# A gated cross-attention and expert layer on one core: from the fourth quad on the third product goes ahead of the fourth, and VectorE's last sums and ScalarE's second Silu take the same order

## The chip, the core and the metric

The kernel runs on one core of one Trainium2 chip. The metric is the device time of one execution in microseconds (us). Engines are named as the profile names them: PE is TensorE's matmul (PEld its weight load), DVE is VectorE, ACT is ScalarE, POOL is GpSimd, SP is SyncE, which issues the transfers.

## The reference

```python
x = x + tanh(g_xattn) * xattn(layernorm(x), ctx, wq, wk, wv, wo)   # x: 8 x 256 x 512
x = x + tanh(g_ffn) * ffn(layernorm(x), ...)
# ffn, N = 2048 tokens, G = 8 groups, inner width 352, hidden width 512:
xg = x[:, None, :] + einsum('ngi,ghi->ngh', soft, mask_up_w)
g = einsum('ngh,gih->ngi', xg, gate_proj_w)
u = einsum('ngh,gih->ngi', xg, up_proj_w)
a = silu(g) * u
d = einsum('ngi,ghi->ngh', a, down_proj_w)
y = einsum('ng,ngh->nh', scalar, d)
```

The attention part and the routing (softmax over 64 experts, the best 8, shares within each group) come first and are not touched. The change lies in the feed-forward part, in the two projections `g` and `u`, in `silu(g) * u`, and around the projection back (`down`).

## The kernel before

**Tiling.** Every fp32 product is made of three matmuls on a high and a low part of each operand (hi by lo, lo by hi, hi by hi). The feed-forward part goes over the 2048 tokens in two passes of 1024. In each pass it goes through 11 units of inner rows, and each unit is two quads (`j` = 0 and 1), so there are 44 quads, q = 0 to 43: the first pass has q 0 to 21, the second q 22 to 43. Even quads have `j` = 0, odd ones `j` = 1. The first and last two quads are also special in places.

**One quad.** Gate and up projections of 128 inner rows and two 512-token halves are computed with seven block products (a Strassen-like scheme) in place of eight. Each product is six matmuls of 128x512; four times a quad, one more matmul (`soft_product`) adds the group's mask part. The products collect in three PSUM banks A, B, C (banks 2, 3, 0 for even q, and 1, 4, 5 for odd q). PE's order in a quad is: product 1 (A), product 6 (B), the mask products (C, first pass only), product 2 (A), product 5 (C), product 7 (B), two soft matmuls (C, A), two `down` groups of six matmuls each ("early" ones, for all quads but q 0 to 2 and q 43), product 4 and its soft matmul (B), product 3 and its soft matmul (C), and the rest of the quad's four `down` groups. Product 4 waits for DVE's third sum (`s_s3`, "sum3"), product 3 for the sum after it (`s_c22`).

**DVE in a quad** (`for quad in quads` of the vector block), with the lines of the profile: `second_sum` (L1393, needed by product 7), in the first pass the mask tile `a_tile` (L1354, L1357, L1363, L1365, needed by product 5 and by the soft matmuls), the third sum (L1432), `c22` (L1439), the early residual additions `add_down` (L1381, one per `down` group; it frees bank 6 or 7), in the first pass pieces of the routing and of the second pass's token sums (L1385), then `c21` (L1486, needs product 4), `prod` (L1491), the first `scaled` (L1374), `c12` (L1498, needs product 3), `add_down`, `second_activations` (L1400 and the second L1374, which need the second Silu), and the fourth `add_down`, here or after the next quad's `second_sum`.

**ACT in a quad**: `first_sum` (L959), the high part of the previous quad's second activation block (`act_high`, L928), in even quads the high part of the previous unit's down weights (`down_weights`, L942), the next quad's weights in three groups (`weight_high`, L823: after product 2, after product 7, and group C after product 3), the first Silu (L1020), the second Silu (L1042, after `c12`) and `act_high` of the first block (L928).

**POOL in a quad**: in even quads the low parts of the previous unit's down weights (L716), then the low parts of the previous quad's two activation blocks (`act_low`, L721), the low parts of the next quad's weights (L670) in the three groups, and four sums of the weights of the quad after (L659 to L664). In a `down` group PE reads both parts of both quads' activation blocks of a unit: in an even quad the first early `down` is the first to read the unit that has just ended, and waits for POOL's down weights and for `act_low` of the odd quad's first block:

```python
                if t == 0:
                    pe.wait_ge(s_wd_lo, 2 * u + 2)
                if t % 4 == 0:
                    pe.wait_ge(s_at_lo, 4 * u + 2 + c + 1)
                if n >= 2:
                    pe.wait_ge(s_res, n - 1)
```

All order is written out by hand, engine by engine, with semaphores between engines. No scheduler moves anything.

## Time and profile before

| | before |
|---|---|
| median of 3 runs (lowest, highest) | 1060.4 us (1060.38, 1063.29) |
| the profiled execution: its own time, its span | 1062.4 us, 1060.6 us |
| granted TensorE clock | 0.998 |
| busy: PE, DVE, POOL, ACT | 99%, 70%, 58%, 37% of the span |
| chain that ended last, by engine | PE 86%, DVE 10% |

The profiled execution is one run, 2.0 us above the median of the others; its span is the time from its first to its last instruction. A row of the timeline gives start and duration in us, the engine, the line, the operation, and in brackets how long the engine was idle before it and for whom it waited. Matmuls of 128x512 follow each other every 0.23 us although each is shown with 0.39 us, since they are pipelined.

### The profile page before, as it was taken

What the parts mean: (1) busy time and instruction counts of PE and PEld (TensorE: products, weight loads), DVE (VectorE), ACT (ScalarE), POOL (GpSimd) and SP (SyncE); (2) the same over time, 40 slices, a digit from 0 to 9 for tenths busy, and PEclk for the clock granted to TensorE, in tenths of its full rate; (3) what the DMA queues carried; (4) which work ended last, traced back from release to release, by engine and by line L of the source; (5) the groups of instructions that cost most, each with busy time, mean ns of one, the idle gap of its engine ahead of it and who ended that gap; (6) DMA issues with size and microseconds to landing.
All of it is one profiled execution on the core that took longest, in us unless ns stands there. A gap on an engine that the chain in (4) does not pass through costs nothing.

```text
span 1060.6 us, 14525 instructions
## 1 busy us (share of the span) xinstructions
PE 1048.0 (99%) x5394; PEld 890.6 (84%) x5394; DVE 746.3 (70%) x1315; ACT 389.5 (37%) x651; POOL 616.2 (58%) x545
## 2 busy tenths in 40 slices
PE   8999999999999999999999999999999999999998
PEld 8989988988988888888877888888888888888887
DVE  7874655676677887788798888765566565666655
ACT  5334324334434435343334342333332333332331
POOL 2112102122435986778877987777668677668661
PEclk9999999999999999999999999999999999999999
DMA  9212226255796305124236323593321211221202
GB/s 331 77 40 99 61 50 150 61 135 144 239 245 201 129 28 73 53 76 38 92 117 77 123 97 99 179 290 110 115 75 48 75 62 41 75 75 47 75 28 80
DMA packets 114277, 111.64 MB, mean 105 GB/s; under 512 B 20896, under 2 KB 96672, under 8 KB 114208
## 3 DMA queue, kind: packets, MB, share of 16 engines
q1 hardware_dynamic: 113840, 110.58, 36.3%
q8 instruction: 43, 0.70, 0.3%
q14 instruction: 26, 0.21, 0.1%
q10 hardware_dynamic: 368, 0.15, 0.1%
HBM read 79.05 MB, written 31.65 MB: 104 GB/s over the span
## 4 chain that ended last, share of the span: by engine, by line
PE 86%; DVE 10%; issue 2%; ACT 1%; DMA 1%; SPq 0%; DVEq 0%
PE bank L89 37%; PE bank L1728 32%; PE bank L1541 9%; PE bank L1734 4%; PE bank L1560 2%; DVE tmp L1374 1%; DVE a_stack L1365 1%; PE bank L1742 1%; DVE a_stack L1363 1%; DVE xres L1381 1%; DVE a_tmp L1357 1%; DVE tmp L1491 1%; PE bank L1612 1%; DVE tmp L1400 1%; DMA w_raw<-in_w_qkvo 1%
## 5 line engine op out<-in xcount | busy, mean ns | idle before, releaser
L1728 PE MATMUL bank<-x2t,wgu_hi 128*128 128x512 f32 x1144 | 353.0, 390 | 0.0
L670 POOL TENSOR_TENSOR wgu_lo<-wgu_raw,wgu_hi 128x768 fp32r<-128x768 f32 (+2 forms) x143 | 216.7, 1527 | 79.3 <-ACT wgu_hi L823 77.9
L1728 PEld LDWEIGHTS bank<-x2t,wgu_hi 128*128 128x128 f32 x1144 | 214.9, 188 | 44.3
L1728 PE MATMUL bank<-x2t,wgu_lo 128*128 128x512 f32 x572 | 224.4, 392 | 1.1 <-DVE tmp L1432 0.8
L823 ACT CAST wgu_hi<-wgu_raw 128x512 fp32r<-128x512 f32 (+1 forms) x129 | 93.6, 726 | 223.1 <-PE bank L1734 185.3
L1381 DVE TENSOR_TENSOR xres<-xres,bank 128x512 f32<-128x512 f32 x175 | 119.4, 683 | 49.8 <-PE bank L89 49.3
L89 PE MATMUL bank<-wd_hi,at_second 128*128 128x512 f32 x336 | 130.8, 389 | 0.0
L1728 PEld LDWEIGHTS bank<-x2t,wgu_lo 128*128 128x128 f32 x572 | 107.4, 188 | 24.7 <-issue 1.6
L1374 DVE TENSOR_TENSOR tmp<-tmp,scalars 128x512 f32<-128x512 f32 x88 | 101.9, 1158 | 3.0
L642 POOL TENSOR_TENSOR kt_lo<-ctxt_raw,kt_hi 128x256 fp32r<-128x256 f32 x32 | 23.4, 764 | 137.6 <-ACT kt_hi L831 137.6
L89 PE MATMUL bank<-wd_hi,at_first 128*128 128x512 f32 x256 | 100.0, 390 | 0.7 <-issue 0.5
L716 POOL TENSOR_TENSOR wd_lo<-wd_raw,wd_hi 128x512 fp32r<-128x512 f32 x42 | 54.5, 1317 | 59.5 <-ACT wd_hi L942 59.5
L1432 DVE TENSOR_TENSOR tmp<-tmp,bank 128x512 f32<-128x512 f32 x44 | 30.2, 686 | 71.6 <-PE bank L1728 71.2
L89 PEld LDWEIGHTS bank<-wd_hi,at_second 128*128 128x128 f32 x336 | 63.1, 188 | 13.3
L1541 PE MATMUL bank<-xnt_hi,w_hi_qkv 128*128 128x256 f32 x256 | 72.5, 287 | 1.5 <-ACT xnt_hi L773 1.5
L1541 PE MATMUL bank<-xnt_hi,w_lo_qkv 128*128 128x256 f32 x256 | 72.5, 288 | 0.0
L1541 PE MATMUL bank<-xnt_lo,w_hi_qkv 128*128 128x256 f32 x256 | 68.4, 286 | 0.0
L1734 PE MATMUL bank<-soft_t,a_stack 128*128 128x512 f32 x176 | 62.6, 396 | 3.8 <-DVE a_stack L1365 3.7
L1020 ACT ACTIVATE tmp<-bank 128x512 f32<-128x512 f32 x44 | 26.4, 599 | 108.0 <-PE bank L1734 108.0
L89 PE MATMUL bank<-wd_lo,at_second 128*128 128x512 f32 x168 | 65.4, 389 | 0.0
L721 POOL TENSOR_TENSOR at_second<-tmp,at_second 128x512 fp32r<-128x512 f32 x44 | 60.1, 1386 | 5.7 <-ACT at_second L928 5.7
L721 POOL TENSOR_TENSOR at_first<-tmp,at_first 128x512 fp32r<-128x512 f32 x33 | 45.1, 1367 | 24.6 <-ACT at_first L928 24.6
(219 smaller groups left out, 2252.3 us busy)
## 6 DMA issues: line engine op xcount, KB each, us to landing
wgu_raw<-in_w_gate_up SPq DMA_DIRECT2D x43, 512.0 KB, 4.1
wd_raw<-in_w_down SPq DMA_DIRECT2D x22, 512.0 KB, 5.0
a_stacks<-a_stack SPq DMA_DIRECT2D x22, 192.0 KB, 1.9
a_stack<-a_stacks SPq DMA_DIRECT2D x22, 192.0 KB, 4.0
ctxt_raw<-in_ctx_t SPq DMA_DIRECT2D x8, 512.0 KB, 11.7
ctx_raw<-in_ctx SPq DMA_DIRECT2D x8, 512.0 KB, 8.5
x<-x_raw SPq DMA_DIRECT2D x8, 512.0 KB, 8.2
sums_raw<-x SPq DMA_DIRECT2D x16, 256.0 KB, 3.5
```

The source lines that it names most:

```text
L89: last = nc.tensor.matmul(out, stationary, moving, start=n == 0, stop=n == len(pairs) - 1)
L670: last = nc.gpsimd.tensor_tensor(wgu_lo[:, part], raw_of(quad)[:, part], f32(wgu_hi[:, part]), ALU.subtract)
L716: nc.gpsimd.tensor_tensor(lo[:, j], wd_raw[:, j], f32(hi[:, j]), ALU.subtract).then_inc(s_wd_lo, 1)
L721: nc.gpsimd.tensor_tensor(lo, tmp[quad.set][:, SUM_3 if c else ACTED], f32(hi), ALU.subtract).then_inc(s_at_lo, 1)
L823: nc.scalar.copy(wgu_hi[:, group], raw_of(quad)[:, group]).then_inc(s_fw_hi, 1)
L1020: nc.scalar.activation(sums[:, ACTED], psum_a[:], ACT.Silu).then_inc(s_silu_0, 1)
L1374: nc.vector.tensor_tensor(part, part, scalars[:, quad.j, c], ALU.mult).then_inc(s_act, 1)
L1381: nc.vector.tensor_tensor(row, row, bank[6 + t % 2][:], ALU.add).then_inc(s_res, 1)
L1432: nc.vector.tensor_tensor(sums[:, SUM_3], sums[:, SUM_1], psum_b[:], ALU.add).then_inc(s_s3, 1)
L1541: last = nc.tensor.matmul(bank[b0 + e // 2][:, (e % 2) * S:(e % 2 + 1) * S], stationary, moving, start=n == 0, stop=n == len(pairs) - 1)
L1728: last = nc.tensor.matmul(out_bank[:], stationary, moving, start=begins and n == 0, stop=n == len(pairs) - 1, skip_group_check=True)
L1734: return nc.tensor.matmul(out_bank[:], a_stack[:, quad.j, m, :], soft_t[:, quad.j, c, :], start=False, stop=True, skip_group_check=True)
```

## The change

From q = 3 on, PE does product 3 ahead of product 4. DVE's `c12` goes ahead of its `c21`, and ACT's second Silu ahead of the cast of weight group C. What waited for the end of product 3 as the quad's last product now waits for both. `act_high` of the first block comes last in all these quads.

```diff
+def third_first(q):
+
+    return q >= 3
...
                     sp.wait_ge(s_m3, q)
+                    sp.wait_ge(s_m4, q)
...
                 if q == QUADS - 1:
                     down_weights(UNITS - 1)
+                if third_first(q):
+                    second_silu()
                 if after:
                     eng.wait_ge(s_m3, q + 1)
+                    eng.wait_ge(s_m4, q + 1)
                     weight_high(after, 2, GROUP_C)
-                if quad.j == 1:
+                if third_first(q):
                     act_high(quad, 0)
-                eng.wait_ge(s_c12, q + 1)
-                nc.scalar.activation(sums[:, SUM_2], sums[:, SUM_2], ACT.Silu).then_inc(s_silu_1, 1)
-                if quad.j == 0:
-                    act_high(quad, 0)
+                else:
+                    if quad.j == 1:
+                        act_high(quad, 0)
+                    second_silu()
+                    if quad.j == 0:
+                        act_high(quad, 0)
...
                 if q >= 2:
                     dve.wait_ge(s_m3, q - 1)
+                    dve.wait_ge(s_m4, q - 1)
...
+                def last_sum():
+                    dve.wait_ge(s_m3, q + 1)
+                    nc.vector.tensor_tensor(sums[:, SUM_2], sums[:, SUM_2], psum_c[:], ALU.add).then_inc(s_c12, 1)
+
+                if third_first(q):
+                    last_sum()
                 dve.wait_ge(s_m4, q + 1)
                 nc.vector.tensor_tensor(sums[:, SUM_1], sums[:, SUM_1], psum_b[:], ALU.add).then_inc(s_c21, 1)
...
-                dve.wait_ge(s_m3, q + 1)
-                nc.vector.tensor_tensor(sums[:, SUM_2], sums[:, SUM_2], psum_c[:], ALU.add).then_inc(s_c12, 1)
+                if not third_first(q):
+                    last_sum()
...
             def product_3(quad):
                 q, psum_c = quad.q, banks_of(quad)[2]
+                pe.wait_ge(s_fw_lo, 3 * q + 3)
                 pe.wait_ge(s_c22, q + 1)
...
+                if third_first(q):
+                    product_3(quad)
                 product_4(quad)
-                product_3(quad)
+                if not third_first(q):
+                    product_3(quad)
```

On DVE this stood between the end of quad 41's early additions and quad 42's `second_sum` (tmp_1 holds the sums of odd quads, xres the output rows, bank4 is B and bank5 is C):

```order
L1486 TENSOR_TENSOR tmp_1_141<-tmp_1_141,bank4 128x512 [waits m4_ready]
L1491 TENSOR_TENSOR tmp_1_141<-tmp_1_141 128x512 [waits silu0_done,c21_done]
L1374 TENSOR_TENSOR tmp_1_141<-tmp_1_141,scalars_149 128x512 [waits prod_done]
L1498 TENSOR_TENSOR tmp_1_141<-tmp_1_141,bank5 128x512 [waits m3_ready]
L1381 TENSOR_TENSOR xres_49<-xres_49,bank6 128x512 [waits down_ready]
L1400 TENSOR_TENSOR tmp_1_141<-tmp_1_141 128x512 [waits c22_done,silu1_done]
L1374 TENSOR_TENSOR tmp_1_141<-tmp_1_141,scalars_149 128x512 [waits prod_done]
L1393 TENSOR_TENSOR tmp_0_140<-tmp_0_140,bank3 128x512 [waits m6_ready,sum1_done]
```

and this stands there now:

```order
L1503 TENSOR_TENSOR tmp_1_141<-tmp_1_141,bank5 128x512 [waits m3_ready]
L1508 TENSOR_TENSOR tmp_1_141<-tmp_1_141,bank4 128x512 [waits m4_ready]
L1513 TENSOR_TENSOR tmp_1_141<-tmp_1_141 128x512 [waits silu0_done,c21_done]
L1390 TENSOR_TENSOR tmp_1_141<-tmp_1_141,scalars_149 128x512 [waits prod_done]
L1397 TENSOR_TENSOR xres_49<-xres_49,bank6 128x512 [waits down_ready]
L1416 TENSOR_TENSOR tmp_1_141<-tmp_1_141 128x512 [waits c22_done,silu1_done]
L1390 TENSOR_TENSOR tmp_1_141<-tmp_1_141,scalars_149 128x512 [waits prod_done]
L1409 TENSOR_TENSOR tmp_0_140<-tmp_0_140,bank3 128x512 [waits m6_ready,sum1_done]
```

The sum that reads bank5 (`c12`) has moved from the fourth place to the first, and the two scaled products (`prod`, `scaled`) begin one place later, behind the end of product 4, which is now the quad's last.

On ACT, from quad 41's group C weights on to the down weights of quad 42 (at_second0 and at_second1 are the two activation blocks of an odd quad), before:

```order
L823 CAST wgu_hi_118<-wgu_raw1_145 128x768 [waits wgu_sums,m7_ready]
L823 CAST wgu_hi_118<-wgu_raw1_145 128x512 [waits wgu_sums,m3_ready]
L928 CAST at_second0_155<-tmp_1_141 128x512 [waits down_ready,act_ready]
L1042 ACTIVATE tmp_1_141<-tmp_1_141 128x512 [waits c12_done]
L959 COPY tmp_0_140<-bank2 128x512 [waits prod_done,m1_ready]
L928 CAST at_second1_156<-tmp_1_141 128x512 [waits down_ready,act_ready]
L942 CAST wd_hi_150<-wd_raw_147 128x512 [waits down_ready,wd_in]
L942 CAST wd_hi_150<-wd_raw_147 128x512
```

and now:

```order
L829 CAST wgu_hi_118<-wgu_raw1_145 128x768 [waits wgu_sums,m7_ready]
L1042 ACTIVATE tmp_1_141<-tmp_1_141 128x512 [waits c12_done]
L829 CAST wgu_hi_118<-wgu_raw1_145 128x512 [waits wgu_sums,m4_ready,m3_ready]
L934 CAST at_second0_155<-tmp_1_141 128x512 [waits down_ready,act_ready]
L965 COPY tmp_0_140<-bank2 128x512 [waits prod_done,m1_ready]
L934 CAST at_second1_156<-tmp_1_141 128x512 [waits down_ready,act_ready]
L948 CAST wd_hi_150<-wd_raw_147 128x512 [waits down_ready,wd_in]
L948 CAST wd_hi_150<-wd_raw_147 128x512
```

The Silu moved from behind the first block's cast to ahead of group C. The order of the four rows from L959 (L965 now) on is the same.

On PE, in quad 43, the last one, which has no early `down` groups, before (bank4 is B, bank5 is C):

```order
L1734 MATMUL bank5<-soft_t_146,a_stack_148 128x512 [waits a_loaded1]
L1734 MATMUL bank1<-soft_t_146,a_stack_148 128x512
L1728 MATMUL bank4<-x2t_139,wgu_lo_119 128x512 [waits sum3_done,wgu_lo_done]
L1728 MATMUL bank4<-x2t_139,wgu_hi_118 128x512 x2
L1728 MATMUL bank4<-x2t_139,wgu_lo_119 128x512
L1728 MATMUL bank4<-x2t_139,wgu_hi_118 128x512 x2
L1734 MATMUL bank4<-soft_t_146,a_stack_148 128x512
L1728 MATMUL bank5<-x2t_139,wgu_lo_119 128x512 [waits c22_done]
L1728 MATMUL bank5<-x2t_139,wgu_hi_118 128x512 x2
```

and now:

```order
L1756 MATMUL bank5<-soft_t_146,a_stack_148 128x512 [waits a_loaded1]
L1756 MATMUL bank1<-soft_t_146,a_stack_148 128x512
L1750 MATMUL bank5<-x2t_139,wgu_lo_119 128x512 [waits c22_done,wgu_lo_done]
L1750 MATMUL bank5<-x2t_139,wgu_hi_118 128x512 x2
L1750 MATMUL bank5<-x2t_139,wgu_lo_119 128x512
L1750 MATMUL bank5<-x2t_139,wgu_hi_118 128x512 x2
L1756 MATMUL bank5<-soft_t_146,a_stack_148 128x512
L1750 MATMUL bank4<-x2t_139,wgu_lo_119 128x512 [waits sum3_done,wgu_lo_done]
L1750 MATMUL bank4<-x2t_139,wgu_hi_118 128x512 x2
```

The product that waits for `c22` now follows the soft matmuls directly, and the one that waits for the third sum comes second. In q 3 to 42 the same two products change places, behind the two early `down` groups.

## Rows read from the trace of the kernel before

**Rows 1.** Busy time by stage: first pass, and second pass without its end
```profile
320.00:690.00 370.00, 364.68 (x1691) 300.20 (x1690) 305.87 (x442) 142.30 (x223) 288.69 (x239) 1.00 0.38 98
690.00:1029.00 339.00, 339.00 (x1490) 279.07 (x1489) 211.20 (x278) 116.83 (x192) 248.45 (x212) 1.00 0.27 86
```

**Rows 2.** Waits of PE over the whole span: us in total, times, longest
```profile
PE bank L1734 <- DVE a_stack L1365: 3.7, 8, 0.9
```

**Rows 3.** Waits of PE between 500 and 660 us (quads 11 to 19)
```profile
PE bank L1734 <- DVE a_stack L1365: 3.3, 6, 0.9
```

**Rows 4.** Timeline of PEld and PE, first `down` of quad 40
```profile
989.16 0.19 PEld L89 LDWEIGHTS bank<-wd_hi,at_first 128*128 128x128 f32 x1
...
989.31 0.39 PE L89 MATMUL bank<-wd_hi,at_first 128*128 128x512 f32 x1
```

**Rows 5.** Timeline of POOL from quad 39 to 40
```profile
980.17 1.60 POOL L670 TENSOR_TENSOR wgu_lo<-wgu_raw,wgu_hi 128x512 fp32r<-128x512 f32 x1
985.29 2.55 POOL L716 TENSOR_TENSOR wd_lo<-wd_raw,wd_hi 128x512 fp32r<-128x512 f32 x2 [3.52 <-ACT wd_hi L942]
987.80 2.55 POOL L721 TENSOR_TENSOR at_second<-tmp,at_second 128x512 fp32r<-128x512 f32 x2
```

**Rows 6.** Timeline of ACT from quad 39 to 40
```profile
979.47 0.62 ACT L823 CAST wgu_hi<-wgu_raw 128x512 fp32r<-128x512 f32 x1 [4.57 <-PE bank L1734]
...
983.59 0.59 ACT L959 COPY tmp<-bank 128x512 f32<-128x512 f32 x1 [1.71 <-PE bank L1728]
984.07 0.62 ACT L928 CAST at_second<-tmp 128x512 fp32r<-128x512 f32 x1
984.59 1.15 ACT L942 CAST wd_hi<-wd_raw 128x512 fp32r<-128x512 f32 x2
```

**Rows 7.** Timeline of DVE from quad 39 to 40
```profile
977.88 0.69 DVE L1486 TENSOR_TENSOR tmp<-tmp,bank 128x512 f32<-128x512 f32 x1 [0.90 <-PE bank L1734]
978.60 0.86 DVE L1491 TENSOR_TENSOR tmp<-tmp 128x512 f32<-128x512 f32 x1
979.50 1.12 DVE L1374 TENSOR_TENSOR tmp<-tmp,scalars 128x512 f32<-128x512 f32 x1
980.54 0.68 DVE L1498 TENSOR_TENSOR tmp<-tmp,bank 128x512 f32<-128x512 f32 x1
981.13 0.68 DVE L1381 TENSOR_TENSOR xres<-xres,bank 128x512 f32<-128x512 f32 x1
981.91 0.69 DVE L1400 TENSOR_TENSOR tmp<-tmp 128x512 f32<-128x512 f32 x1
982.64 0.69 DVE L1374 TENSOR_TENSOR tmp<-tmp,scalars 128x512 f32<-128x512 f32 x1
985.05 0.69 DVE L1393 TENSOR_TENSOR tmp<-tmp,bank 128x512 f32<-128x512 f32 x1 [1.72 <-PE bank L1728]
```

**Rows 8.** Timeline of POOL and DVE in quad 38, one operation of each
```profile
965.16 1.30 POOL L670 TENSOR_TENSOR wgu_lo<-wgu_raw,wgu_hi 128x512 fp32r<-128x512 f32 x1
...
965.90 1.10 DVE L1400 TENSOR_TENSOR tmp<-tmp 128x512 f32<-128x512 f32 x1
```

**Rows 9.** Timeline of DVE in quad 43
```profile
1036.88 0.69 DVE L1432 TENSOR_TENSOR tmp<-tmp,bank 128x512 f32<-128x512 f32 x1 [2.73 <-PE bank L1728]
1037.61 0.69 DVE L1439 TENSOR_TENSOR tmp<-tmp,bank 128x512 f32<-128x512 f32 x1
...
1042.84 0.68 DVE L1381 TENSOR_TENSOR xres<-xres,bank 128x512 f32<-128x512 f32 x1
```

**Rows 10.** Timeline of PEld and PE in quad 43, around products 4 and 3
```profile
1037.69 0.19 PEld L1728 LDWEIGHTS bank<-x2t,wgu_lo 128*128 128x128 f32 x1 [0.81 <-issue]
...
1037.72 0.47 PE L1728 MATMUL bank<-x2t,wgu_lo 128*128 128x512 f32 x1 [0.42 <-DVE tmp L1432]
...
1040.78 0.39 PE L1734 MATMUL bank<-soft_t,a_stack 128*128 128x512 f32 x1
...
1043.73 0.39 PE L89 MATMUL bank<-wd_hi,at_first 128*128 128x512 f32 x1
```

More of the change, by code:

```diff
@@ L1033, in _, with second_silu @@
                     x2_whole(B - 1, 6)
+                def second_silu():
+                    eng.wait_ge(s_c12, q + 1)
+                    nc.scalar.activation(sums[:, SUM_2], sums[:, SUM_2], ACT.Silu).then_inc(s_silu_1, 1)
                 if q == QUADS - 1:
                     down_weights(UNITS - 1)
+                if third_first(q):
+                    second_silu()
                 if after:
                     eng.wait_ge(s_m3, q + 1)
+                    eng.wait_ge(s_m4, q + 1)
                     weight_high(after, 2, GROUP_C)
-                if quad.j == 1:
+                if third_first(q):
                     act_high(quad, 0)
-                eng.wait_ge(s_c12, q + 1)
-                nc.scalar.activation(sums[:, SUM_2], sums[:, SUM_2], ACT.Silu).then_inc(s_silu_1, 1)
-                if quad.j == 0:
-                    act_high(quad, 0)
+                else:
[4 more added lines that the diff above has]
+                        act_high(quad, 0)
             act_high(quads[-1], 1)
```

## The prediction, made before the changed kernel ran

> **What bounds the kernel now.** I read the busy time by stage first, to see which engine fills each stage. In the second pass PE is busy for all 339.00 us of 339.00, at the full clock; in the first pass for 364.7 of 370.0 [rows 1]. The reader is to see there that nothing can be gained in the second pass by a new order, since PE does the same matmuls, and that anything that makes PE wait is lost in full. Then the waits of PE: the largest is 3.7 us in eight waits of the soft matmuls for DVE's mask tile [rows 2], and 3.3 us of it, six waits, falls in quads 11 to 19 [rows 3], where DVE also does routing and token sums. This is all that a change of DVE's order could win there. Then the timeline over one boundary from an odd to an even quad, engine by engine, to see how much room the chain behind DVE has.
>
> It has none. In quad 40 (even), the first weight load of `down` stands at 989.16 and its matmul at 989.31, a lead of 0.15 us [rows 4]. POOL's two `act_low` take 2.55 us from 987.80, so the first, which this load waits for, ends at about 989.08; the load follows within 0.1 us. Followed back: POOL has just done the low parts of the down weights, and was idle for 3.52 us before them, waiting for ACT's down weights [rows 5]; ACT started these at 984.59, directly behind the cast of quad 39's second block at 984.07 [rows 6]; and that cast needs DVE's second `scaled` of quad 39, which ends at 982.64 + 0.69 = 983.33 [rows 7]. So DVE has 0.7 us of room at that one place, and everything behind it (0.52 us to the down weights, then two weight parts and one block on POOL) is a fixed chain to a load of PE that is just in time. The second pass has 11 even quads (22 to 42), all with this pattern at one period of 15.9 us per quad.
>
> **What each part costs.** *On PE, quads 3 to 42*: the same matmuls, two products exchanged. Product 3 now comes right after the early `down` groups and needs `c22`; these groups are 12 matmuls, 2.7 us, and DVE's `c22` follows the third sum by 0.7 us, so they cover it. Without that cover each of 40 quads would lose about 0.7 us, 29 us. Cost 0. *The added waits* (one more semaphore on PE, DVE, ACT and SP) are for events that PE has long passed, or, for group C on ACT and the mask stack on SP, for the same moment as before, the end of the quad's last product. Cost 0.
>
> *On DVE*, `c12` moves up and `c21`, `prod`, `scaled` move behind the end of both products. That end is seen at 979.47, where ACT's group C cast starts [rows 6]; the end of the first of the two is at 977.88, where `c21` starts now [rows 7]. So `c12` takes the place at 977.88, DVE idles from 978.57 to 979.47, and from there the chain is `c21`, `prod`, `scaled`, `add_down`, `prod` of the second block, second `scaled`. Steps between starts are read off the rows: 0.72 from `c21` to `prod` (977.88 to 978.60), 0.59 from `c12` to the next independent operation (980.54 to 981.13), 0.73 from L1400 to L1374 (981.91 to 982.64) [rows 7]. With nothing else in the way: 979.47, 980.19, 980.92, 981.52, 982.11, 982.84, end at 983.53. That is inside the 0.7 us of room.
>
> But `prod` and `scaled` read two tiles of SBUF each, and POOL's subtraction for group C starts at 980.17 [rows 5], in the same hundredths as `prod` at 980.19. What that does is seen in quad 38: POOL's subtraction runs from 965.16 to 966.46, and DVE's L1400, started at 965.90, takes 1.10 us in place of 0.69 and ends 0.54 us after POOL's end, as if it had run only when POOL was done [rows 8]. `c21` and the other sums out of PSUM show 0.68 or 0.69 throughout and are not touched. Before, DVE's `scaled` at 979.50 met the group C subtraction and POOL waited (1.60 us in place of 1.30), while `c12` and `add_down` ran beside it and the last two operations found POOL idle [rows 5, 7]. Now, if POOL is first: it ends at 980.17 + 1.30 = 981.47, `prod` at 982.01, `scaled` runs 982.05 to 982.74, then 982.64, 983.23, and the second `scaled` from 983.96 to 984.65. ACT's cast, before at 984.07, comes at 984.68: 0.61 us late. If DVE is first: POOL's subtraction ends 1.15 us after `prod` (as 981.77 after 980.62), at 982.03, `scaled` at 982.57, and the whole is 0.17 us earlier: 0.44 us late. The down weights, POOL's three operations and PE's load then move by 0.44 to 0.61. Of this PE takes all but 0.05: it can lose the 0.15 us lead down to the 0.03 us seen where it does wait (load 1037.69, matmul 1037.72 [rows 10]), but resumes with a slower first step (0.30 us in place of 0.23). So 0.39 to 0.56, middle 0.48, in 11 quads: **5.2 us lost**. From even to odd quads the same delay meets only `second_sum`, which product 7 needs some 2 us after it now starts, and costs nothing.
>
> On whether the lock is for the whole operation the Trainium skill, page "SBUF — State Buffer", section "Who interferes with whom", has a harsher rule: a DVE instruction with two SBUF inputs and a GpSimd instruction that reads SBUF exclude each other, and the loser fully blocks for the whole instruction of the other. By it L1400 would end 0.69 us after POOL in quad 38, not 0.54; by the rule the 11 quads would lose some 1.6 us more than by the row. The trace agrees that they exclude each other, and I go by its 0.54.
>
> *Quad 43* has no early `down` groups. PE's load for product 4 comes at 1037.69, 0.08 us after `c22` has begun, that is when the third sum is done; now it waits for `c22`, which starts and ends 0.73 us after the third sum (1036.88 and 1037.61) [rows 9, 10]. Behind it, the first `add_down` frees the bank for the third `down` group. It starts at 1042.84 and ends at 1043.52; that group's first matmul is at 1043.73, its load 0.2 earlier, so this too is just in time. Now `c21` starts at the end of the last product, 1040.78 + 0.39 for the last matmul, 0.03 for the signal and 0.73, that is 1041.93, and `add_down` 0.72 + 0.73 + 0.59 later, ending at 1044.65 where 1044.25 would keep pace; less the little lead of the load, 0.3 us. Sum **1.0 us lost** (0.7 to 1.3).
>
> *First pass, quads 11 to 19.* Here DVE is last for the soft matmuls. Four odd-to-even boundaries (into 12, 14, 16, 18) meet the same collision with group C; I charge each 0.5, 2.0 us. Against it stands the wait for the Silu: now L1400 starts 0.78 us after `add_down`, and would start 0.59 after it [rows 7], which gives back 0.19 at about five boundaries, 0.9. Net **1.1 us lost**. Bounds: only the gain, -0.9; collisions on every boundary at 0.9 and a weaker gain, +3.5. Quads 3 to 10 and 20 have room, by the few waits there.
>
> *Sum*: 5.2 + 1.0 + 1.1 = 7.3 us. The profiled execution of 1062.4 us (span 1060.6) becomes 1069.7; against the median of 1060.4 us it is **1067.7 us**. Bounds of this case: 4.3 + 0.7 - 0.9 = 4.1 and 6.2 + 1.3 + 3.5 = 11.0, so 1064.5 to 1071.4.
>
> **Rivals.** *Hidden*: the group C subtraction lets `prod` pass, or the cast keeps its 0.7 us of room. For it: the chain without a collision ends at 983.53. Against: the two starts coincide within 0.02 us, and either order of them costs. It leaves the end and the first pass: 1.0 to 2.1, 1061.4 to 1062.5 us, no difference that can be told from none (0.3%, 3.2 us, is about what a measurement tells).
>
> *Faster*: the earlier Silu takes the mask tile off PE's path in quads 11 to 19. Place: the six waits of [rows 3]; price: with the earlier two the whole 3.7 us [rows 2], and in quad 43 nothing lost. That gives 1056.7 us. It decides only if DVE reaches its mask tile 0.9 us earlier (the longest wait) with no collision in the second pass. Against: 0.19 us per quad is all that the Silu gives.
>
> *Much slower*: the delay at even quads adds a second collision, POOL's `act_low` against DVE's last two operations, and the delayed `second_sum` reaches product 7. Each takes up to 0.5 us more in 11 quads: 5.5 us on top, 1073.2 us or more. Against: 2 us of room before product 7.
>
> **How the numbers follow.** Forecast 0.76, hidden 0.14, faster 0.04, much slower 0.06. Predicted is the forecast's 1067.7. The range runs from the lower rival's 1061.5 to 1072.5, past the bound of 1071.4, and leaves out some 2 in 10. Slower by over 0.3% (above 1063.6): 0.76 and 0.06, less 0.02 for a forecast at its low bound, 0.80; within it 0.16; faster 0.04.
>
> **What would show it.** Right: in even quads from 22 on PE idles about 0.5 us ahead of the first L94 (before L89) matmul, released by POOL's `act_low`; ACT's cast of down weights in quad 40 starts about 0.6 us later after product 1 of its quad; DVE's `prod` or `scaled` in odd quads takes 1.2 to 1.8 us beside POOL; PE waits 1.1 us, not 0.4, in quad 43. The second pass no longer shows PE busy throughout. Wrong: PE stays without waits between 690 and 1029 us; or the mask tile's waits of 3.3 us shrink or grow by more than 2 us; or waits appear at product 3 in quads with early `down` groups.

## The result and the profile after

| | before | changed |
|---|---|---|
| median of 5 runs (lowest, highest) | 1060.42 us (1060.38, 1063.68) | 1072.06 us (1067.92, 1074.36) |
| the profiled execution: its own time, its span | 1062.4 us, 1060.6 us | 1072.06 us, 1070.2 us |

The ratio is 1.0092, with a 95% interval of 1.0075 to 1.0109: the change makes the kernel about 0.9% slower; the medians differ by 11.6 us, the profiled spans by 9.6 us. Here and below a ratio compares fast runs, and one run of experiment 6, of 4994.37 us, is left out of its ratio as slow. The ratios of the experiments are to runs of the kernel before that were taken with them, whose medians were 1061.62 us (experiments 1 to 4) and 1061.64 us (6 and 11); the changed kernel was not run again beside them. Busy time of the changed kernel, from its page:

```profile
PE 1051.5 (98%) x5394; PEld 888.9 (83%) x5394; DVE 762.8 (71%) x1315; ACT 391.7 (37%) x651; POOL 615.0 (57%) x545
```

Its windows by stage, in the columns of [rows 1]:

```profile
320.00:690.00 370.00, 361.63 (x1673) 296.61 (x1672) 315.17 (x438) 140.53 (x221) 285.69 (x237) 1.00 0.37 96
690.00:1029.00 339.00, 336.18 (x1466) 274.07 (x1465) 210.85 (x272) 116.54 (x189) 243.21 (x209) 1.00 0.27 87
```

PE is no longer busy throughout the second pass (336.18 of 339.00, before all of it), and in the first pass it has lost 3 us. The clock is full in both. Waits of PE over the whole span, those in the two passes:

```profile
PE bank L1756 <- DVE a_stack L1381: 5.7, 11, 0.8
PE bank L94 <- issue: 2.5, 12, 0.5
...
PE bank L1750 <- DVE tmp L1455: 1.1, 1, 1.1
PE bank L1647 <- DVE xres L1397: 1.0, 2, 0.5
PE bank L1750 <- DMA x2t<-x2l: 1.0, 1, 1.0
...
PE bank L1624 <- DVE xres L1397: 0.3, 1, 0.3
```

There is more of the wait of [rows 2] (5.7 us in place of 3.7), and five kinds are new or larger. The 12 short ones at L94 name no engine; what they are is read from the engines around one, below.

To see *where* the time went I use DVE's third sum, which comes once a quad. Its starts in quads 1, 11, 22 and 23 of the kernel before (quad 43's is in [rows 9]):

```profile
338.44 0.69 DVE L1432 TENSOR_TENSOR tmp<-tmp,bank 128x512 f32<-128x512 f32 x1
...
509.78 0.69 DVE L1432 TENSOR_TENSOR tmp<-tmp,bank 128x512 f32<-128x512 f32 x1 [1.56 <-PE bank L1728]
...
702.06 0.69 DVE L1432 TENSOR_TENSOR tmp<-tmp,bank 128x512 f32<-128x512 f32 x1 [2.73 <-PE bank L1728]
...
718.02 0.69 DVE L1432 TENSOR_TENSOR tmp<-tmp,bank 128x512 f32<-128x512 f32 x1 [2.73 <-PE bank L1728]
```

and in quads 1, 11, 22, 23 and 43 of the changed one:

```profile
336.89 0.69 DVE L1448 TENSOR_TENSOR tmp<-tmp,bank 128x512 f32<-128x512 f32 x1
...
511.58 0.68 DVE L1448 TENSOR_TENSOR tmp<-tmp,bank 128x512 f32<-128x512 f32 x1
...
704.72 0.69 DVE L1448 TENSOR_TENSOR tmp<-tmp,bank 128x512 f32<-128x512 f32 x1 [2.73 <-PE bank L1750]
...
722.35 0.69 DVE L1448 TENSOR_TENSOR tmp<-tmp,bank 128x512 f32<-128x512 f32 x1 [2.38 <-PE bank L1750]
...
1045.44 0.69 DVE L1448 TENSOR_TENSOR tmp<-tmp,bank 128x512 f32<-128x512 f32 x1 [2.38 <-PE bank L1750]
```

The stretches between them, and the same taken from each experiment's profile, as difference to the kernel before in us (q1 to q11 before is 509.78 - 338.44 = 171.34; after 511.58 - 336.89 = 174.69, so +3.35):

| | start to q1 | q1 to q11 | q11 to q22 | q22 to q23 | q23 to q43 | q43 to end |
|---|---|---|---|---|---|---|
| before, length | 338.44 | 171.34 | 192.28 | 15.96 | 318.86 | 23.72 |
| changed | -1.55 | +3.35 | +0.86 | +1.67 | +4.23 | +1.04 |
| second_only | -1.37 | 0.00 | -0.19 | +0.67 | +4.29 | +1.10 |
| first_only | -1.70 | +2.60 | -1.34 | +0.44 | +0.03 | +0.07 |
| even_only | -1.30 | +2.82 | -1.50 | +0.67 | +0.01 | +0.10 |
| odd_only | -1.45 | -0.20 | +2.45 | +0.43 | +4.30 | +1.07 |
| weights_ahead | +3.04 | +2.47 | +0.52 | +0.72 | -0.20 | +1.15 |
| small_c | -1.05 | +2.61 | +0.86 | +0.73 | -0.02 | +1.07 |
| but_22 | -1.25 | +3.26 | +0.93 | +0.43 | +4.30 | +1.13 |
| adds_early | -1.60 | +1.78 | +0.11 | +1.04 | +4.29 | +1.08 |
| pe_only | -0.77 | +7.47 | +5.42 | +1.36 | +15.40 | +1.72 |
| mended | -2.05 | +0.82 | +0.47 | -0.02 | -0.20 | +0.08 |
| before_weights_ahead | -1.37 | +0.84 | -0.65 | -0.03 | -0.19 | +0.10 |

The first column is work ahead of everything the kernels differ in. It moves by -2.1 to +3.0 us from one profiled execution to the next, so no reason hangs on it, and a span alone doesn't tell these kernels apart. The last two columns repeat within 0.11 us wherever the code is the same; these carry verdicts. The first pass stands between: a quad there repeats only where no near tie is decided in it (below).

**One boundary of the second pass**, from quad 41 to 42, in the changed kernel. DVE:

```profile
1017.86 0.69 DVE L1503 TENSOR_TENSOR tmp<-tmp,bank 128x512 f32<-128x512 f32 x1 [0.90 <-PE bank L1756]
1019.45 0.69 DVE L1508 TENSOR_TENSOR tmp<-tmp,bank 128x512 f32<-128x512 f32 x1 [0.90 <-PE bank L1756]
1020.17 0.69 DVE L1513 TENSOR_TENSOR tmp<-tmp 128x512 f32<-128x512 f32 x1
1020.90 1.66 DVE L1390 TENSOR_TENSOR tmp<-tmp,scalars 128x512 f32<-128x512 f32 x1
...
1023.79 0.69 DVE L1390 TENSOR_TENSOR tmp<-tmp,scalars 128x512 f32<-128x512 f32 x1
```

POOL, ACT, and PE's load and matmul:

```profile
1020.19 1.82 POOL L676 TENSOR_TENSOR wgu_lo<-wgu_raw,wgu_hi 128x512 fp32r<-128x512 f32 x1 [0.48 <-ACT wgu_hi L829]
1025.74 2.54 POOL L722 TENSOR_TENSOR wd_lo<-wd_raw,wd_hi 128x512 fp32r<-128x512 f32 x2 [3.73 <-ACT wd_hi L948]
1028.25 2.54 POOL L727 TENSOR_TENSOR at_second<-tmp,at_second 128x512 fp32r<-128x512 f32 x2
...
1019.49 0.62 ACT L829 CAST wgu_hi<-wgu_raw 128x512 fp32r<-128x512 f32 x1 [0.28 <-PE bank L1756]
...
1024.52 0.63 ACT L934 CAST at_second<-tmp 128x512 fp32r<-128x512 f32 x1 [0.36 <-DVE tmp L1390]
1025.05 1.14 ACT L948 CAST wd_hi<-wd_raw 128x512 fp32r<-128x512 f32 x2
...
1029.61 0.19 PEld L94 LDWEIGHTS bank<-wd_hi,at_first 128*128 128x128 f32 x1 [0.58 <-issue]
...
1028.84 0.61 PE L1756 MATMUL bank<-soft_t,a_stack 128*128 128x512 f32 x2
1029.64 0.47 PE L94 MATMUL bank<-wd_hi,at_first 128*128 128x512 f32 x1 [0.18 <-issue]
1029.94 0.39 PE L94 MATMUL bank<-wd_lo,at_first 128*128 128x512 f32 x1
```

and in the kernel before, ahead of the matmul of [rows 4]:

```profile
988.86 0.62 PE L1734 MATMUL bank<-soft_t,a_stack 128*128 128x512 f32 x2
```

It is read from the top. `prod` (1020.17) is 0.02 us ahead of POOL's subtraction (1020.19); in the odd quads 23 to 41 it is ahead every time, by 0.02 or 0.03 us in nine and by 0.30 us in quad 25. POOL takes 1.82 us (1.30 when nothing holds it up, 1.60 at the same place before), `scaled` 1.66 (0.69 and 1.12). All is then counted from ACT's group C cast. Down weights come 5.56 us after it (1025.05 - 1019.49; before 984.59 - 979.47 = 5.12 [rows 6]), POOL's `act_low` 8.76 after (8.33 before [rows 5, 6]), PE's load 10.12 after (9.69 before [rows 4, 6]): 0.43 or 0.44 us late at each step, down to PE's load. On PE, from the start of the two soft matmuls to the first L94 matmul it is 0.80 us (1029.64 - 1028.84) where it was 0.45 (989.31 - 988.86): 0.35 us lost. The step behind it is 0.30 in place of 0.23, another 0.07, together 0.42. These quads' period is 16.36 to 16.40 us, before 15.93 to 15.97. The view of waits shows 0.18 us, less than half of that. The other quads from 24 on keep their period.

**Quads 43 and 22**, first matmul of the product that waits:

```profile
709.29 0.47 PE L1750 MATMUL bank<-x2t,wgu_lo 128*128 128x512 f32 x1 [0.97 <-DMA x2t<-x2l]
...
1046.99 0.47 PE L1750 MATMUL bank<-x2t,wgu_lo 128*128 128x512 f32 x1 [1.14 <-DVE tmp L1455]
```

The second is the forecast wait for `c22` (1.14 us; before, the first matmul of the product in that place waited 0.42 us for the third sum [rows 10]). The first was not forecast: product 3 of quad 22 waits for a block of the second pass's tokens.

### The profile page after: what moved, and what is told of

Its sections match the earlier page's. It is cut to its first block, busy times and chain, and to the rows that moved or that the text cites. A ratio compares the mean times of both kernels' runs of the same rounds, so it can differ in the third digit from the quotient of the medians.

```text
span 1070.2 us, 14609 instructions
## 1 busy us (share of the span) xinstructions
PE 1051.5 (98%) x5394; PEld 888.9 (83%) x5394; DVE 762.8 (71%) x1315; ACT 391.7 (37%) x651; POOL 615.0 (57%) x545
## 4 chain that ended last, share of the span: by engine, by line
PE 83%; DVE 12%; issue 3%; DMA 2%; SPq 0%; ACT 0%; DVEq 0%
PE bank L94 36%; PE bank L1750 30%; PE bank L1563 9%; PE bank L1756 4%; PE bank L1582 2%; DVE a_stack L1381 2%; DVE xres L1397 1%; DVE a_tmp L1372 1%; DMA x2t<-x2l 1%; DVE tmp L1390 1%; DVE a_stack L1379 1%; PE bank L1764 1%; DVE tmp L1416 1%; PE bank L1634 1%; DVE tmp L1513 1%
## 5 line engine op out<-in xcount | busy, mean ns | idle before, releaser
L676 POOL TENSOR_TENSOR wgu_lo<-wgu_raw,wgu_hi 128x768 fp32r<-128x768 f32 (+2 forms) x143 | 224.6, 1583 | 77.3 <-ACT wgu_hi L829 77.3
L94 PE MATMUL bank<-wd_hi,at_second 128*128 128x512 f32 x336 | 130.9, 389 | 0.0
L1390 DVE TENSOR_TENSOR tmp<-tmp,scalars 128x512 f32<-128x512 f32 x88 | 122.1, 1388 | 3.0
L94 PE MATMUL bank<-wd_hi,at_first 128*128 128x512 f32 x256 | 101.0, 395 | 3.0 <-issue 2.5
L1042 ACT ACTIVATE tmp<-tmp 128x512 f32<-128x512 f32 x44 | 27.9, 634 | 174.7 <-DVE tmp L1503 174.7
L94 PEld LDWEIGHTS bank<-wd_hi,at_second 128*128 128x128 f32 x336 | 63.1, 188 | 13.4
L727 POOL TENSOR_TENSOR at_first<-tmp,at_first 128x512 fp32r<-128x512 f32 x33 | 49.9, 1511 | 32.1 <-ACT at_first L934 32.1
L94 PE MATMUL bank<-wd_lo,at_second 128*128 128x512 f32 x168 | 65.4, 389 | 0.0
```

Of the source, the lines that this page charges most:

```text
L94: last = nc.tensor.matmul(out, stationary, moving, start=n == 0, stop=n == len(pairs) - 1)
L676: last = nc.gpsimd.tensor_tensor(wgu_lo[:, part], raw_of(quad)[:, part], f32(wgu_hi[:, part]), ALU.subtract)
L727: nc.gpsimd.tensor_tensor(lo, tmp[quad.set][:, SUM_3 if c else ACTED], f32(hi), ALU.subtract).then_inc(s_at_lo, 1)
L1042: nc.scalar.activation(sums[:, SUM_2], sums[:, SUM_2], ACT.Silu).then_inc(s_silu_1, 1)
L1390: nc.vector.tensor_tensor(part, part, scalars[:, quad.j, c], ALU.mult).then_inc(s_act, 1)
```

## The experiments

**1. Second pass alone.**

```diff
 def third_first(q):
-    return q >= 3
+    return q >= 22
```

> The new order in quads 22 to 43 only. Theory: odd to even boundaries lose 0.43 us each in ten quads (24 to 42; quad 22 follows a quad in the old order and loses nothing), 4.3 us, and the end loses 1.0 us: 1065.7 us, plus up to 1 us if the third product of quad 22 still finds its token block late. Rival (the whole loss is one effect of the first pass that carries on): 1060.4 us.

Measured: 1067.14 us (12 runs), ratio 1.0041 [1.0019, 1.0064]. q23 to q43 loses 4.29 us in ten even quads and the end 1.10, as in the full change; the first pass loses nothing.

**2. First pass alone** (`return 3 <= q < 22`).

> The new order in quads 3 to 21 only (first pass); quads 22 to 43 as before. By my theory (losses are tied to places) the second pass goes back to 15.93 us in every quad, the end loses nothing, and what is left is the first pass: about 4 us in the profiled run (from +4 to +5, of which up to 1.2 may be the wait for the token blocks at quad 22), so 1063 to 1066 us. Rival (the prediction's sizes): 1.1 us, 1061.5 us.

Measured: 1065.34 us (12 runs), ratio 1.0026 [1.0008, 1.0043]. The second pass is as before to 0.1 us, apart from its first quad. Its profile was taken from its fastest run (1062.49), so the table shows less than the median: one near tie, described at the end, makes quad 15 in it 1.5 us shorter than in the changed kernel. The medians of experiments 1 and 2 are 5.5 and 3.7 us above those of the kernel before, 9.2 us together, where the full change has 11.6.

**3. PE's order alone**: products exchanged, DVE's `c12` and ACT's Silu where they were.

```diff
-                if third_first(q):
+                if False:
                     last_sum()
...
-                if not third_first(q):
-                    last_sum()
+                last_sum()
```

This is DVE's part; on ACT the second Silu and `act_high` go back to their old places.

> PE's products exchanged as in the change, but DVE's last sum and ACT's second Silu stay where they were before. Theory: what costs is that the sum behind the fourth product and the two SBUF products after it start 1.6 us later; with the third product's sum again behind them the chain to the second scaled part is longer by one sum (0.6 us) and the wait for the Silu (0.2 us), so each even quad of the second pass loses 1.2 us in place of 0.43: some 8 us more than the change, 1080 us, and more in the first pass. Rival (moving the sum up, ahead of the product that collides with POOL, is what costs): faster than the change, near 1061 us.

Measured: 1094.15 us (6 runs), ratio 1.0287 [1.026, 1.0313], more than I expected. The second pass loses 15.40 us, 1.54 in each even quad and the odd one behind it together. ACT and PE from quad 39 into 40, and from 40 into 41:

```profile
1005.35 0.62 ACT L829 CAST wgu_hi<-wgu_raw 128x512 fp32r<-128x512 f32 x1 [4.62 <-issue]
...
1011.69 1.14 ACT L948 CAST wd_hi<-wd_raw 128x512 fp32r<-128x512 f32 x2
...
1027.28 0.58 ACT L965 COPY tmp<-bank 128x512 f32<-128x512 f32 x1
...
1016.27 0.47 PE L94 MATMUL bank<-wd_hi,at_first 128*128 128x512 f32 x1 [0.96 <-issue]
...
1028.00 0.47 PE L1744 MATMUL bank<-x2t,wgu_lo 128*128 128x512 f32 x1
```

The down weights come 6.34 us after group C (before 5.12 [rows 6]), 1.2 us late, for which PE waits. I had not counted the rest: the Silu, held back by the late `c12` (it starts at 1026.23), stands ahead of ACT's `first_sum` (1027.28, done at 1027.86), and PE's next product in that bank starts only at 1028.00, 0.24 us late by the spacing of the matmuls before it (the last two start at 1027.30 and 1027.53), and again with a first step of 0.31 us: some 0.3 us. That the Silu's place does this is read from the rows, not tried. So the moves of `c12` and the Silu together are what keeps the change cheap; which of the two does more was not tried.

**4. The down weights ahead on ACT.** Added to the full change, in even quads: ACT casts them before quad q-1's second block, so that they no longer wait for DVE's last `scaled`.

```diff
+                if quad.j == 0 and u >= 2:
+                    down_weights(u - 1)
                 act_high(quads[q - 1], 1)
-                if quad.j == 0 and u >= 2:
-                    down_weights(u - 1)
```

> The change, and on ACT in even quads the casts of the down weights go ahead of the cast of the second activation block of the quad before, so that they no longer wait for DVE. Theory: the chain DVE, ACT, POOL, PE into even quads gets 0.5 us or more of room and the 0.43 us per even quad of the second pass are gone: all its quads at 15.93 to 15.96 us, 4.7 us faster than the change, 1067 us. Rival (PE waits at that place for something else, the residual additions or a bank): no difference, 1072 us.

Measured: 1067.08 us (12 runs), ratio 1.0045 [1.0027, 1.0062]. ACT and PE at one boundary:

```profile
986.09 0.62 ACT L829 CAST wgu_hi<-wgu_raw 128x512 fp32r<-128x512 f32 x1 [0.28 <-PE bank L1756]
...
990.65 1.14 ACT L948 CAST wd_hi<-wd_raw 128x512 fp32r<-128x512 f32 x2
...
995.88 0.39 PE L94 MATMUL bank<-wd_hi,at_first 128*128 128x512 f32 x1
```

The down weights come 4.56 us after group C in place of 5.56, PE's wait is gone, and q23 to q43 is at -0.20. DVE still collides (its `scaled` takes 1.66 us here too): in the second pass the collision costs only through this chain.

**5. Hardly any POOL subtraction to collide with.** The full change, with the group C subtraction of quads 23 to 43 cut to 8 of its 512 columns. This leaves out part of the weights' low parts.

```diff
+                if quad.q >= 23 and n == 2:
+                    nc.gpsimd.tensor_tensor(wgu_lo[:, W_U1, 0, 0:8], raw_of(quad)[:, W_U1, 0, 0:8],
+                                            f32(wgu_hi[:, W_U1, 0, 0:8]), ALU.subtract).then_inc(s_fw_lo, 1)
+                    return
```

> The change, with POOL's subtraction for weight group C cut to 8 columns of 512 for the weights of quads 23 to 43 (the rest of that low part keeps older values, so part of the computation is left out). Theory: DVE's first scaled product in odd quads of the second pass takes 0.69 us in place of 1.66 us, the second ends 1.0 us earlier, inside the room before ACT's cast, and all second pass quads from 24 on take 15.93 to 15.96 us: 4.3 us less. Rival (the later end of the last product alone makes the chain late): still 0.4 us lost in each even quad.

Measured: one run, 1066.64 us; q23 to q43 is at -0.02. DVE's same operations:

```profile
984.04 0.69 DVE L1394 TENSOR_TENSOR tmp<-tmp,scalars 128x512 f32<-128x512 f32 x1
...
985.96 0.69 DVE L1394 TENSOR_TENSOR tmp<-tmp,scalars 128x512 f32<-128x512 f32 x1
```

`scaled` is back at 0.69. Behind the end of both products there is room for all six operations of DVE when POOL doesn't hold them up. Experiments 4 and 5 cut the same chain in two places, and either removes the loss: for the second pass from quad 24 on it is shown.

**6. The same reordering on the kernel before.**

> The kernel before the change, with only ACT's casts of the down weights moved ahead of the cast of the second activation block. Theory: the first down group of the even quads gets 0.5 us of room; nothing waits for it in the second pass before, so only the 0.5 us wait in quad 14 can go: 0 to 1 us faster, 1060 us. Rival: the later cast of the activation block holds the residual chain, slower.

Measured: 1061.67 us (12 runs), ratio 0.9992 [0.9976, 1.0008]: the same. Where PE's load was just in time, more room gives next to nothing: 0.19 us in ten even quads (15.93 us each in place of 15.93 to 15.97). In the first pass the 0.46 us wait into quad 15 is gone, and PE has two new waits of 0.60 us for `xres` ahead of its routing, into quads 5 and 9, which were not expected.

**7. Quad 22 left at the old order** (`q >= 3 and q != 22`).

> The change, but quad 22, the first of the second pass, keeps the fourth product ahead of the third. Theory: the last token block of the second pass is read 1.6 us later, so the wait of 1.0 us of PE for it in quad 22 is gone, and the period of the quad 22 to 23, 17.63 us in the changed kernel, falls to 16.4 us (the 0.43 us of the late activation block stays). Rival: the transfers are late by more than a product and the wait only moves to the other product.

Measured: one run, 1071.16 us. q22 to q23 is 16.39 us in place of 17.63, and the DMA wait is gone from PE's waits. Product 3 of quad 22 reads the block one product (1.6 us) earlier. SP also issues it behind quad 21's product 4 (`s_m4`), which is now that quad's last; but that is not needed for the loss: in experiments 1 and 9 quad 21 keeps the old order, and PE still waits 0.4 us and q22 to q23 still loses 0.67. Whether the later issue adds to it is open, for the size is not fixed: the wait was 0.97 us in the changed kernel's profile, and 0.5 and 0.3 in those of experiments 4 and 8.

**8. The fourth addition early in the first pass.** From quad 3 on, where the next quad has routing on PE, DVE does the quad's fourth `add_down` at once and not behind the next `second_sum`.

```diff
-    return q in (12, 13)
+    return q in (12, 13) or q >= 3 and q + 1 in ROUTED_ON_ODD
```

> The change, and in the quads ahead of a quad with routing work on PE (3, 4, 5, 7, 8, 9, 12, 17) DVE's fourth residual addition goes ahead of the second activations. Theory: PE's three waits for that addition ahead of the routing matmuls (two of 0.5 us and one of 0.3 us in the changed kernel) vanish, 1.3 us; the 0.43 us per even quad of the second pass stay; waits for the mask tile stay within 1 us of 5.7 us. Rival: the waits for the mask tile grow by as much, since DVE does the same work before it.

Measured: one run, 1069.12 us. The waits of L1647 (1.0 us) and L1624 (0.3) for `xres` are gone, and q1 to q11 loses 1.78 us in place of 3.35. This 1.6 us is a net figure and not the price of those waits. Into quads 5 and 9, where the L1647 waits stood, the periods go from 17.60 to 17.95 and from 18.07 to 17.90. Quad 7, ahead of which no addition was moved, gets 0.96 us shorter and its wait for the mask tile is gone; quad 11 gets 0.39 longer. The waits for the mask tile fall from 5.7 to 4.3 us, more than the 1 us allowed for. Quad 4 is even 0.7 us shorter than before the change (17.31 against 18.02), and the early addition was not tried on the kernel before, so part of the 1.6 us may be a gain that has nothing to do with the change.

**9 and 10. Even quads alone, and odd quads alone** (`q >= 3 and q % 2 == 0`, `... == 1`).

> The new order in even quads from 4 on only. Theory: entering odd quads stays as in the change: quads 5, 7, 9 and 11 are 0.4, 1.1, 0.4 and 1.1 us longer than before, 3.0 us together; the second pass has 15.93 to 15.96 us in every quad from 24 on, and the end (quad 43, an odd one) 23.7 us as before. Rival: the second pass still loses 0.43 us in every second quad.

> The new order in odd quads from 3 on only. Theory: a quad pays for the order of the quad ahead of it, so entering even quads stays as in the change (0.43 us for each even quad of the second pass, 4.3 us over quads 23 to 43, and the end 1.0 us), and entering odd quads is as before: quads 5, 7, 9 and 11, which are 0.4, 1.1, 0.4 and 1.1 us longer in the changed kernel than before, go back to 17.19, 16.85, 17.63 and 16.84 us. Rival (a quad pays for its own order): they stay long, and the even quads are free.

Measured: one run each, 1063.17 and 1069.03 us. Quad periods in the first pass, us, worked out from the third sums:

```
quad    before  changed  odd_only  even_only
q5      17.19   17.60    17.16     17.63
q7      16.85   17.93    16.85     17.93
q9      17.63   18.07    17.63     18.06
q11     16.84   17.92    16.85     17.92
```

Odd quads pay for the order of the even quad ahead: 3.0 us in these four. In quads 5 and 9 PE waits 0.48 and 0.49 us for the fourth addition, in 7 and 11 it waits 0.54 us each for the mask tile. In the second pass it is the other way round: even_only +0.01, odd_only +4.30. What an odd quad meets, from quad 6 to 7 of the changed kernel:

```profile
429.94 1.66 DVE L1390 TENSOR_TENSOR tmp<-tmp,scalars 128x512 f32<-128x512 f32 x1
...
432.83 1.67 DVE L1390 TENSOR_TENSOR tmp<-tmp,scalars 128x512 f32<-128x512 f32 x1
...
437.20 2.24 DVE L1381 TENSOR_TENSOR a_stack<-a_tmp,a_stack 32x384 fp32r<-32x384 f32 x1
...
432.33 1.62 POOL L727 TENSOR_TENSOR at_first<-tmp,at_first 128x512 fp32r<-128x512 f32 x1 [1.28 <-ACT at_first L934]
...
439.49 0.74 PE L1756 MATMUL bank<-soft_t,a_stack 128*128 128x512 f32 x2 [0.54 <-DVE a_stack L1381]
```

and the second `scaled` and the last operation of the mask tile at the same place before:

```profile
432.92 0.69 DVE L1374 TENSOR_TENSOR tmp<-tmp,scalars 128x512 f32<-128x512 f32 x1
...
437.37 0.55 DVE L1365 TENSOR_TENSOR a_stack<-a_tmp,a_stack 32x384 fp32r<-32x384 f32 x1
```

Before, the two `scaled` took 1.12 and 0.69 us, and the last operation of the mask tile 0.55. Now both meet POOL, the second at `act_low`, and the mask tile slides into POOL's subtraction and takes 2.24 us. In the second pass the two `scaled` of an even quad are held up just as much (1.67 and 1.68 us, at 1005.02 and 1007.92), but there is no mask tile, and nothing waits for this delay.

The stretch from quad 11 to 22 shows the reverse of the first: odd_only loses 2.45 us there and even_only gains 1.50, with quad 15 at 19.70 and 19.48 us, so that the tie below is not the cause. Most of the gain is quad 13. Before, DVE's cast in the mask tile was held up there (1.60 us) and PE waited; in the changed kernel the cast takes 0.36 us and PE has no such wait. The kernel before, then the changed one:

```profile
542.93 1.60 DVE L1363 CAST a_stack<-a_tmp 128x384 fp32r<-128x384 f32 x1 [0.48 <-DVE a_tmp L1357]
...
545.17 0.72 PE L1734 MATMUL bank<-soft_t,a_stack 128*128 128x512 f32 x2 [0.91 <-DVE a_stack L1365]
```

```profile
544.39 0.36 DVE L1379 CAST a_stack<-a_tmp 128x384 fp32r<-128x384 f32 x1
```

Quad 13's period is 17.04 to 17.08 us in the eight profiles where quad 12 has the whole change, and 17.98 or 17.99 in the four where it has the old order (19.05 with PE's order alone). So the change also wins 0.95 us there, and the 0.86 us lost between quads 11 and 22 is a balance of gains and losses.

**11. All three repairs**: experiments 4 and 8, and the change at quads 3 to 42 without 22.

> The change with all places mended that I can name: down weights ahead on ACT, the fourth addition early ahead of quads with routing, quads 22 and 43 left in the old order. Theory: of the changed kernel's loss over its whole length (1070.2 against 1060.6 us of span) the second pass gives back 4.7 us, quad 22 1.2 us, the end 1.0 us, the routing waits 1.3 us, and what is left is some 2 to 3 us of the mask tile in quads 11 to 21: span 1061 to 1065 us, median 1062 to 1066 us. Rival (the sites do not add up, the loss moves to others): over 1068 us.

Measured: 1063.73 us (12 runs), ratio 1.001 [0.9994, 1.0026]: no difference clear of the noise by the ratio, but the median is still 2.1 us above that of the kernel before (1061.64). In the second pass and at the end each new wait is gone and the stretches are as before to 0.2 us. In the first pass the waits for routing are gone, but those for the mask tile are not (6.2 us; 3.7 before, 5.7 in the changed kernel). The profile is of the fastest run (1061.49), in which quad 15 takes 18.35 us against 19.70 before; the stretches of the first pass together are 1.3 us longer than before, and 2.6 us with quad 15 left out. That fits the 2 to 3 us of the mask tile that were expected to remain.

## Why the prediction was right, and where it was not

It gave 1067.7 us (1061.5 to 1072.5), and slower with a chance of 0.80. Measured was 1072.06. That lies inside the range by 0.4 us, and two of the five runs are above 1072.5. It is beyond 1071.4, where the upper bounds of the prediction's own terms end: only the wider range that was drawn around them holds it, and that part is luck.

*Second pass, 5.2 us in 11 even quads: right in mechanism and nearly in size.* Quads 24 to 42 lost 4.23 us, 0.42 each, and quad 22 some 0.43: 4.7 us. `prod` came first at the shared port, by 0.02 us; that case had been put at 0.44 us late, and 0.43 to 0.44 stands at each step. The one error of size is the middle taken between the two orders of start. That PE takes all but 0.05 of it was a little too hopeful: its period loses 0.42. The sign named for it, an idle PE of about 0.5 us released by POOL, shows as 0.18 us for "issue"; the sign of PE's 339 us no longer being full, and that of `scaled` at 1.2 to 1.8 us, came as written.

*The lock.* `scaled` ended 0.55 us after POOL's subtraction (1020.90 + 1.66 = 1022.56, and 1020.19 + 1.82 = 1022.01), as the 0.54 of [rows 8]. The Trainium skill, page "SBUF — State Buffer", section "Summary: rules for kernel authors", says that a DVE operation with two SBUF inputs and a GpSimd operation that reads SBUF exclude each other, and that the second to issue blocks until the first has finished. Read as the whole 0.69 us still to come at that moment, the end would be 0.69 us behind POOL's. The trace agrees that it blocks, and puts the end 0.14 us earlier than this reading, with times of POOL that the profile gives only roughly.

*Quad 43, 1.0 us: right.* 1.04 measured at the end, and the wait ahead of the first of the two products grew from 0.42 us (for the third sum) to 1.14 (for `c22`), 0.72 of the forecast 0.73; with quad 43 at the old order (first_only, even_only, mended) the end loses 0.07 to 0.10.

*The cover of `c22` in quads 3 to 42, cost 0: right.* No such wait shows in any quad with early `down` groups.

*First pass, 1.1 us: this failed.* Measured was 3.35 + 0.86 = 4.2 us, beyond the +3.5 given as its bound (in both profiles the tie in quad 15, described below, went to POOL). The step that fell is "Quads 3 to 10 and 20 have room, by the few waits there". Few waits of PE say that its needs were met, not how early; DVE had less room there than the delay. With it fell "from even to odd quads the same delay meets only `second_sum`", which holds in the second pass and not in the first, where the mask tile and the fourth addition come behind `second_sum` (experiments 9 and 10: 3.0 us in quads 5, 7, 9 and 11). I had written the rule from second-pass rows and applied it to both. For quads 11 to 19 the 1.1 us is near the 0.86 measured between quads 11 and 22, but by luck: odd_only loses 2.45 us there and even_only gains 1.50, sizes that no term of the forecast has.

*The added waits, cost 0: wrong in one place.* SP's added wait was not the trouble. The forecast left out that product 3 of quad 22 reads a token block that has only just been transferred, and now reads it one product earlier. With quad 22 at the old order this loss, about 1.2 us in the changed kernel's profile (1.67 less the 0.43 of the chain), is gone (experiment 7).

*The rivals.* "Hidden" and "faster" fell with the second pass (experiments 1, 4, 5). "Faster" was right that part of the mask tile's wait can go: the longest of the six waits, 0.91 us, is gone in quad 13. That it is the earlier Silu that does it was not tried, and new waits for the mask tile elsewhere outweigh it (4.7 us in place of 3.3 [rows 3] between quads 11 and 19). "Much slower" described its second collision rightly; it happens in both passes, but in the second there is the room that was held against this rival, and only in the first does it cost.

What stays open: the medians are farther apart (11.6 us) than the profiled spans (9.6 us), the kernel before's profile being one of its slower runs, and the changed kernel's runs spread over 6.4 us. How much of that spread is which tie in the first pass was not settled. All first-pass sizes are of one profiled execution each. The early addition alone on the kernel before, and `c12` and the Silu moved one without the other, were not run.

## What to carry to other kernels

Exchanging two pieces of work on the busiest engine costs nothing on it, and delays or advances every event tied to either: list all that wait for each (here DVE's sums, a cast, a reuse of a buffer by a transfer) and follow each to the next use on the busy engine, in every stage of the program and not in one as an example. An engine that is busy 100% of a stage shows nothing of how late its inputs come; measure that lead at each input before counting on room. Where two engines share a port, an order that moves one against the other by a few tenths of a us is a change of their durations too.

## What the hardware did that I had not expected

**A near tie can decide 1.5 us.** In quads 14 to 15 DVE's low part of the token sums and POOL's first weight sum start within 0.01 us of each other. The changed kernel, then first_only:

```profile
569.66 1.83 DVE L1401 TENSOR_TENSOR sums_lo<-sums_raw,sums_hi 128x1024 fp32r<-128x1024 f32 x1
...
569.67 0.73 POOL L665 TENSOR_TENSOR wgu_raw<-wgu_raw 128x256 f32<-128x256 f32 x1
```

```profile
568.74 1.21 DVE L1401 TENSOR_TENSOR sums_lo<-sums_raw,sums_hi 128x1024 fp32r<-128x1024 f32 x1
...
568.74 1.80 POOL L665 TENSOR_TENSOR wgu_raw<-wgu_raw 128x256 f32<-128x256 f32 x1
```

In one POOL goes first and DVE is held up, in the other the reverse; the quad's period is 19.49 us in the first and 17.98 in the second, with the same code in this stretch. Of the eight profiles with the whole change in quad 14, the five where POOL goes first have 19.48 or 19.49 us and the three where DVE does have 17.98 to 18.35. With quad 14 in the old order the tie alone does not decide: where DVE goes first, second_only has 19.70 us and before_weights_ahead 18.43, and where POOL does, the kernel before and odd_only have 19.70. It is a likely source of the spread between runs of one kernel (1067.9 to 1074.4 us); no run isolated it.

**A wait in the view is not the loss.** The view counts PE's idle time from the shown end of the last matmul, 0.39 us behind its start, while the next could have started 0.23 us behind it. So of a gap of 0.35 us it shows 0.18, and the slower first step (0.30 us in place of 0.23) not at all: 0.42 us lost. Eleven such quads show as 2.0 us of waits in the second pass and cost 4.7.
